# Splitting x into a high and a low half in a projection stage: subtraction on PE with a copy on ScalarE, against a subtraction on VectorE

## The reference, cut to what matters

```python
y = attended @ w_proj
x = x + layernorm(y)
xn = layernorm(x)
scores = sigmoid(xn @ router_weight.T)
_, top_idx = top_k(scores + expert_bias, 6)
probs = chosen scores / (sum of chosen scores + 1e-20)
```

## Time and profile before

| | |
|---|---|
| median of 3 runs | 3262.55 us (3261.11, 3262.55, 3276.6) |
| the profiled execution's own time | 3258.48 us |
| span of its trace, first to last instruction | 3256.8 us |
| busy over the span | PE 87%, DVE 68%, ACT 49%, POOL 22% |
| the changed stage, first to last block | about 1105 to 1349 us of the span |
| busy in 1105 to 1350 us | PE 179.1, DVE 186.5, ACT 103.9, POOL 73.0 of 245.0 us |

### The profile page before, as it was taken

How to read it: one execution, slowest core, us unless ns; L and a number is a source line. 1 busy time by engine, 2 the same in 40 slices (tenths; PEclk the granted TensorE clock), 3 DMA queues, 4 the chain that set the end, 5 groups by cost and what they waited for, 6 DMA issues and landing times. The chain is left out here.

```text
span 3256.8 us, 59136 instructions
## 1 busy us (share of the span) xinstructions
PE 2842.0 (87%) x20033; PEld 2062.9 (63%) x20033; DVE 2225.7 (68%) x6134; ACT 1603.0 (49%) x2446; POOL 731.5 (22%) x882
## 2 busy tenths in 40 slices
PE   7959999999999387689947777998399999999998
PEld 6834444444444276578836664555388888888887
DVE  6768999999997388663338883444466666666664
ACT  3506777777777244333325544544244444444443
POOL 1022222222222133247744422222000000000000
PEclk9959999999999666699968888999699999999999
DMA  6984556666662377648857867653432424243331
GB/s 244 330 153 83 108 115 112 112 112 116 112 110 65 127 270 269 214 138 225 221 165 269 296 228 228 183 162 100 132 99 74 122 65 117 78 102 92 90 86 46
DMA packets 342662, 485.87 MB, mean 149 GB/s; under 512 B 58832, under 2 KB 203248, under 8 KB 342384
## 3 DMA queue, kind: packets, MB, share of 16 engines
q1 hardware_dynamic: 331776, 468.94, 52.1%
q0 software_dynamic: 10240, 14.16, 2.3%
q10 hardware_dynamic: 496, 0.84, 0.1%
HBM read 278.77 MB, written 204.53 MB: 148 GB/s over the span
## 5 line engine op out<-in xcount | busy, mean ns | idle before, releaser
L551 ACT ACTIVATE att_pr<-att_e_ps 128x1024 f32<-128x1024 f32 (+2 forms) x640 | 567.3, 938 | 203.8 <-PE att_e_ps L603 203.8
L579 PE MATMUL att_m_ps<-att_ks,att_qs 63*128 63x512 f32 (+3 forms) x1536 | 465.9, 433 | 40.2 <-PEq L41 31.7
L513 DVE CUSTOM_DVE_ANT_0 att_kept<-att_m_ps,att_causal 128x256 f32<-128x256 f32 (+3 forms) x1024 | 448.5, 488 | 50.3 <-DVEq L41 21.9
L579 PEld LDWEIGHTS att_m_ps<-att_ks,att_qs 63*128 63x128 f32 x1536 | 234.3, 189 | 370.6 <-DVE att_mx L516 148.5
L492 POOL TENSOR_SCALAR_AFFINE_SELECT att_pr<-att_pr 128x256 f32<-128x256 f32 (+1 forms) x384 | 181.4, 485 | 698.0 <-PEq L594 694.5
L516 DVE TENSOR_REDUCE att_mx<-att_m_ps 128x1 f32<-128x512 f32 x512 | 323.3, 684 | 21.5 <-PE att_m_ps L579 17.5
L623 PE MATMUL att_o_ps<-att_pr,att_vs 128*32 128x512 f32 (+3 forms) x3072 | 328.7, 501 | 3.7 <-issue 2.0
L2604 ACT ACTIVATE fin_hh<-fin_hid 128x512 fp32r<-128x512 f32 x192 | 121.4, 632 | 399.8 <-DVE fin_hid L2450 302.2
L603 PE MATMUL att_e_ps<-att_qs,att_ks 64*128 64x512 f32 (+3 forms) x1536 | 269.1, 376 | 6.7 <-ACT att_pr L551 3.3
L2343 POOL TENSOR_TENSOR fin_rs<-fin_ve,fin_mhalf 128x4 f32<-128x4 f32 x48 | 48.4, 1007 | 928.6 <-POOLq L41 928.6
L2446 DVE TENSOR_TENSOR fin_hid<-fin_gate,fin_u_ps 128x512 f32<-128x512 f32 x192 | 131.5, 685 | 136.4 <-ACT fin_gate L2598 82.9
(11 more groups left out here) (332 smaller groups left out, 6921.2 us busy)
## 6 DMA issues: line engine op xcount, KB each, us to landing
fin_raw<-weights SPq DMA_DIRECT2D x32, 1024.0 KB, 9.6
att_qs<-q_high SPq DMA_DIRECT2D x128, 128.0 KB, 5.2
att_ks<-k_high SPq DMA_DIRECT2D x128, 128.0 KB, 6.5
attended<-att_ot SPq DMA_DIRECT2D x64, 256.0 KB, 8.5
acc<-att_zero SPq DMA_DIRECT2D x64, 256.0 KB, 2.2
moe_w<-w SPq DMA_DIRECT2D x128, 128.0 KB, 3.4
lqk_a<-acc SPq DMA_DIRECT2D x32, 512.0 KB, 6.0
attended<-lin_ot SPq DMA_DIRECT2D x32, 512.0 KB, 3.7
```

What stands on the lines that cost most here:

```text
L513: e.tensor_tensor_reduce(kept[:, n % MBUF, 0:w], m_ps[:, n % MBUF, 0:w], causal[:, BLK - w:], 1.0, -3e38, ALU.add, ALU.max, mx[:, h, at, q ...
L551: e.activation(out, src, ACT.Exp).then_inc(exp_done, 1)
L579: e.matmul(m_ps[:, (2 * i + n) % MBUF, 0:w], qs[rows, j, p, q * P:(q + 1) * P], ks[rows, j, p, h * BLK:h * BLK + w], start=True, stop=True ...
```

## The change

In every slot, for block c, the low half of x is made in another way. PE, after the choice of d, waits for `xh_ready` and multiplies `xh` by a matrix with -1 on its diagonal (`minus`, made once by DVE from the identity), accumulating onto `t_ps`: two fp32r matmuls of 512 columns. ACT, at the end of its list, waits for that (`rest_ready`) and copies `t_ps` to `xl`. The DVE instruction L1052 and its wait go. So that PE can accumulate onto `t_ps`, the 8 transposes become 8 ordinary fp32 matmuls by the identity. Separately, the maximum search runs over the padded `sb`, so that its result holds the padding values and the 6 largest scores; it is used directly, and the copy into `pick` goes with the array.

```diff
         ident = ph.sb("ident", [P, P])
+        minus = ph.sb("minus", [P, P], f32r)
@@ tiles and semaphores
-        pick = ph.sb("pick", [P, TPB, 8])
+        rest_ready = ph.sem("rest_ready")
@@ DVE, before the first slot
                 split_weights(e, step, wf, wh, wl)
+                e.wait_ge(pe_consts, 1)
+                step(e.tensor_scalar(minus[:], ident[:], -1.0, None, ALU.mult))
                 step(e.memset(sb[:, :, E:E + 8 - K], 3e38))
-                step(e.memset(pick[:, :, K:8], 3e38))
@@ DVE, choose
                     for t in range(TPB):
-                        e.max(top[:, t], sb[:, t, 0:E])
+                        e.max(top[:, t], sb[:, t])
                     step.settle()
-                    step(e.tensor_copy(pick[:, :, 0:K], top[:, :, 0:K]))
                     for t in range(TPB):
-                        e.match_replace(rep[:, t], pick[:, t], sb[:, t], -3e38)
+                        e.match_replace(rep[:, t], top[:, t], sb[:, t], -3e38)
@@ DVE, stages
-                    if c is not None:
-                        e.wait_ge(xh_ready, 1)
-                        e.tensor_tensor(xl[:, c[1]], t_ps[:], xh[:, c[1]].bitcast(fp32), ALU.subtract
-                                        ).then_inc(xl_ready, 1)
-                        take(e, (xh_ready, 1))
@@ ACT, stages, after rt
+                    if c is not None:
+                        e.wait_ge(rest_ready, 1)
+                        e.activation(xl[:, c[1]], t_ps[:], ACT.Copy).then_inc(xl_ready, 1)
+                        take(e, (rest_ready, 1))
@@ PE, turn
-                            i = e.transpose(t_ps[:, k, t * P:(t + 1) * P], src[:, t, k * P:(k + 1) * P], ident[:])
+                            i = e.matmul(t_ps[:, k, t * P:(t + 1) * P], src[:, t, k * P:(k + 1) * P], ident[:], start=t == 0,
+                                         stop=t == TPB - 1)
@@ PE, stages, after the choice of d
+                    if c is not None:
+                        e.wait_ge(xh_ready, 1)
+                        for k in range(KC):
+                            i = e.matmul(t_ps[:, k], minus[:], xh[:, c[1], k], start=False, stop=True,
+                                         skip_group_check=True)
+                        i.then_inc(rest_ready, 1)
+                        take(e, (xh_ready, 1))
```

## The result

| | before | changed |
|---|---|---|
| median | 3259.76 us (20 runs, 3252.99 to 3276.6) | 3276.02 us (20 runs, 3263.46 to 3285.29) |
| ratio of the two | | 1.0041, 95% interval 1.0028 to 1.0055 |
| profiled execution, and its span | 3258.48, 3256.8 | 3283.37, 3281.6 us |
| the stage, first to last instruction | 268.7 | 282.7 us |
| mean distance of al, slots 3 to 15 | 13.77 | 14.50 us |

What follows compares the result with a forecast made beforehand. DVE's list of 13.77 us was taken to bound the stage's slots; the change closes a PE-ACT chain of 14.3 us. 13 slots give +7.7, the ends +5, together +12.7 us: 3275 us, range 3256 to 3290.

Steps and rivals of the forecast that it cites:

- DVE no longer sets the slot; PE's rest gates y: Stage slots: PE's wait for xh holds back the next y, closing a chain through PE and ACT; 13.77 becomes 14.3 us.
- The terms: Chain from y through logits, sigmoid, xn, ah, yn, xh, hand-over and rest: 15.25 us at the earlier trace's clock.
- 14.3 us a slot: Stage slot length taken between 13.9 and 14.8 us, within clock bounds of 12.8 and 15.25; 13.77 before.
- The sum and the ends: Slots 3 to 16: 185.9 against 178.2 us, +7.7; slots 2, 16 and 17 about +5; together +12.7 us.
- The turn is hidden: PE's transposes as ordinary matmuls: 3.4 us instead of 2.17, done 0.9 us before xh starts, cost 0.
- The choice of the largest, the copy on ACT, `minus`: nothing: Search over 66 columns costed at nothing, ACT's xl copy beside y, `minus` before slot 0: all hidden.
- DVE's list of 11.45 us: DVE's work per slot falls by 2.32 us, from 13.77 to 11.45, with L1052, L1009 and their waits gone.
- DVE's relief comes through: Rival: y doesn't wait for xh, so slots follow DVE's 11.45 us; -29 + 5, 3238 us; chance 0.04.
- the turn wakes the clock: Rival: ordinary matmuls raise PE's clock, held into rest and y; slots 12.8 to 13.3, 3256 to 3263 us; chance 0.25.
- the clock doesn't help: Rival: rest gates y, clock's rise stays where seen from y; slots 15.25 us, +25, 3288 us; chance 0.18.
- A slip in a bound: Turn's upper bound: 0.41 us per record, 6.6 us, said to pass xh by 1.8 and delay choice and rest nearly 2.

Runs made afterwards that it cites:

- e3: Kernel before, with PE at the end of its slot also waiting for xh, no rest matmuls: 3270.5 us, ratio 1.0032, slot 14.47 us.
- e5: Changed kernel with the rest moved to the next slot, behind y and ahead of the logits: 3253.77 us, ratio to before 0.9983, slot 13.14 us.
- e2: Kernel before with only the eight transposes made ordinary fp32 matmuls: 3274.61 us, ratio 1.0046, slot 13.75 us.
- e1: Kernel before with only the choice's edit (search over the padded scores, no copy into pick): 3259.44 us, ratio 0.9998, slot 13.76 us.
- e7: Changed kernel unaltered, run once more for a second trace: 3268.66 us (one), slot 14.37 us, stage 276.2 us.
- e8: e2 with 39 more already met waits on PE ahead of the first slot, shifting later code: 3262.06 us, ratio to before 1.0015, slot 13.85 us.
- e6: e5 with two PSUM buffers for y, so y needn't wait for ACT's release: 3251.69 us, ratio to before 0.9978, slot 13.15 us.
- e10: e6 with the 1e-20 added as a constant tile by tensor_tensor: 3252.54 us, ratio to before 0.9979, slot 13.15 us.

## Why the prediction was right, point by point

- **DVE no longer sets the slot; PE's rest gates y.** Right, and it is the cause: e3 has the wait alone and 14.47 us; e5 takes the wait from ahead of y and leaves all the work, and the loss is gone.
- **The terms.** From y at 1236.99 to y at 1251.67 us, 14.68: y, logits and hand-over to the sigmoid 7.23 (forecast 7.61 with the clock of the earlier trace rows, some 0.5 less with a clock that rises 5 matmuls earlier), sigmoid to the end of xh 6.38 (6.51), hand-over 0.05 (0.10), rest 1.02 (1.03). Every term held within 0.15 in this kind of slot, for which the working gave 14.8.
- **14.3 us a slot.** 14.50 in the first trace, 14.37 in the second. I took one kind of slot; there are four, and the longest, with y wholly at the low clock, is 14.98 from y to y, where the working had 15.25 with the rest at the low clock too. That slots would move against the clock's rises, and gain by it in some, stood there; that they also lose by it in one of four did not. The step from 14.8 down to 14.3 had no working, so that the mean came within 0.2 of it is partly luck.
- **The sum and the ends.** The two parts were off in opposite directions. From slot 3's y to slot 16's the changed kernel took 188.3 us against 178.2 before, +10.1 (forecast +7.7). What is outside of that gave +3.9 (forecast +5): +2.4 up to slot 3's y (forecast +2.2), +1.9 behind slot 16's (forecast about +3), -0.3 ahead of the first al. Together +14.0. On the second trace's stage it is +7.5. The forecast +12.7 and the ratio's +13.4 agree better than two traces do with each other.
- **The turn is hidden.** Right: e2's slots are 13.75. The size too at the nearest row: at the low clock its records follow one another by 3.36/15 = 0.22 us (forecast 0.213), and there was 0.74 us between the choice and the rest's release.
- **The choice of the largest, the copy on ACT, `minus`: nothing.** Right in the changed kernel, which has slack on DVE. In the kernel before the choice's edit alone gave 0.1 of its 0.22 us at best (e1).
- **DVE's list of 11.45 us.** Wrong, though the forecast didn't hang on it. In e5, where DVE hardly waits for another engine, the slot is 13.14. The step was "13.77 - 2.32": it took every other instruction to stay as it was. The removal moved the addition under POOL's sum, and there it takes 1.75 us more: 11.45 + 1.75 = 13.2. That is the length of the list, not what the stretch costs: in the slot of e5 in which POOL's sum ends at 1237.88 DVE reads that sum from 1238.49 on, so without the stretch it could have been there 0.6 us sooner at most. How short the slots would get is not shown. The rival "DVE's relief comes through" was priced at 3238; the relief that e5 shows is 0.63 us a slot.
- **The rival "the turn wakes the clock".** Partly true. Its price, 12.8 to 13.3, is what the second trace's slots with y at the high clock show (13.00, 13.13), but few slots have it. The Trainium skill (TensorE: Matmul & The Clock Gate, Part 4: PE-mode transpose) says that transposes in transpose mode don't count as PE being busy for the clock. What the prediction had as the trace's side of it, that the clock never held through a turn and no turn ends in a high clock, was a misreading: three of the 16 turns of the kernel before ran at the high clock, and that of 1280.09 us to its end. The traces agree with the page in another way: the clock rises within a turn of ordinary matmuls in the changed kernel (three times), e7 and e8, and within none of transposes in the kernel before, e1 and e3. They don't prove it, since the changed kernel's rises came 3.1 us into the turn and a turn of transposes lasts only 2.17. What decided was the rival's own "against": in half of the slots the clock fell between choice and rest.
- **The rival "the clock doesn't help"** (15.25 a slot): near to one slot in four (14.98).
- **A slip in a bound.** With records of 0.41 us the turn would end about 7.2 us after xn's start, 2.1 behind the start of xh at 5.09, not 1.8. Nothing else hangs on it.

## What to carry to other kernels

Before giving a piece of work to an engine with spare time, look at what stands behind it in that engine's list: the rest costs 1 us of PE, which had it, but its wait held back a y product whose operands had been there for 2.5 us. Behind y, the same operations gain 9 us in the stage where they had cost 14. Read the effect in the distances of the slots of the changed stage, too: five of the traces here (the changed kernel's first, e2, e5, e6, e10) had 9 to 14 us more than the kernel before from a stage that no edit had touched.

## What the runs showed of the hardware that was not expected

- A 128x4 addition on DVE beside POOL's 128x1024 addition took 1.92 us instead of 0.17 and ended with it, within 0.03 us, in two forms; a 128x1024 subtraction with one operand in PSUM was not stretched, nor was the 128x256 reduction just ahead of the addition (0.42 us, started with POOL's sum). The Trainium skill (VectorE: DVE Perf Modes, Two Vector instructions with no wait between them) speaks of a second SBUF read interface that VectorE shares with GpSimd, used by an instruction with two SBUF tensors or in a 2-port perf mode. The instructions stretched and spared here would fit that, and so would the multiplication L1023 of the kernel before, with two SBUF tensors: 0.50 to 0.52 us in the twelve slots in which it begins 0.2 us before POOL's sum ends, else 0.41 to 0.43. But the 128x1024 division L988 (two SBUF tensors) takes no more than 1.26 us beside POOL's 128x4 power of 1.01, against 1.22 alone. That the shared read is the cause is argued, not shown.
- PE's pause at a repeat of the linear attention's loop was 3.7 to 4.3 us in all traces but that of e2, where it was 9.87 us, twice, and 39 more waits ahead of it brought it back. What in the position of the code makes the difference stays open.
- The granted clock of a stage that is the same in all kernels differs between executions: linear attention took 302.3 to 317.1 us in traces with ordinary pauses (e3 and the changed kernel), at a mean clock of 0.88 in the latter. The time of one execution can't tell such a change from none.
